# Scattering token rows to expert slots in the dense stage, and turning rows by DMA instead of TensorE, in a two-layer recurrent block

## The chip, the cores and the metric

The kernel runs on one NeuronCore of a Trainium2 chip. The metric is the device time of one execution in microseconds; the kernel before was timed three times, and one more execution was profiled. TensorE is written PE (its weight loads PEld), VectorE DVE, ScalarE ACT, GpSimd POOL, and SyncE, which issues most of the DMAs, SP.

## The reference

Layer 0 takes 8192 token rows of 256 numbers, normalises them, and runs linear attention (keys and values are summed into one small matrix per batch of 2048 tokens) beside a mixture of 16 experts: each token goes to its two best experts and also through one shared expert. Layer 1 is a retention attention and a feed-forward layer with FP4 quantised weights and activations. The change touches only layer 0:

```python
scores = softmax(xt @ gate_w.T); top_w, top_i = top_k(scores, 2)
# step over the 16 experts, for the tokens that chose this one:
a = silu(x @ W1.T + b1) * (x @ W3.T + b3)        # 127 numbers
h = concat([sqrt(sum(a*a) + 1), a])               # 128 numbers
s = h @ W2.T + b2                                 # 255 numbers
out = concat([sqrt(sum(s*s) + 1), s])             # one row of 256 per token and expert
```

The shared expert is the same computation with an inner width of 256. The attention that reads the key-value sums follows these stages, and a later stage combines for each token its two expert rows (found through `pos_lo` and `pos_hi`, the slots of the token).

## The kernel before

The core works through phases; each ends by clearing its semaphores and a barrier of all engines (`Phase.clear`). Within a phase every engine has a stream of its own, made by `pipeline`: at step s an engine runs, in the listed order, `stage(s - skew)` for each pair (skew, stage). An engine executes its list strictly in order, and stages of different engines meet through semaphores: `done(t)` waits until stage t of the other engine has finished, `free(t)` until the buffer that tile t - 2 used is free (two buffers, `LAG` = 2). Floats are kept as two float16 halves (hi and lo), and a product is three matmuls (`split3`).

Phases around the change, in their order:

- `weights0` loads and splits weights, and POOL fills constants; SP's later copies wait for all fills.
- `phase_norm` normalises the tokens, writes them as float16 halves to `x16_dram` (1 KB for each token) and holds them turned (features on partitions) in `xT_all`.
- `phase_route` chooses the experts and gives each (token, expert) pair a slot. Slots are sorted by expert, and each expert's slots are padded to a multiple of 128: 144 tiles of 128 slots. DVE does all of it in some 50 steps, each waiting for the one before; PE counts once in between.
- `phase_dense`, 64 tiles of 128 tokens: keys, values and key-value sums, and the shared expert (project, square and square root, `turn` on PE, copy `hidden_T` on DVE, `down`, then `z_out` on ACT and a store to `z_dram`). Beside it POOL runs `times` (a clamp at L1202 and a power at L1205, for the inner row of one tile and the outer row of an earlier one) and `scatter`: two indirect DMAs (L1212) that write token numbers, 4 bytes each, to `perm_dram` at the tokens' slots. SP loads a 381.5 KB expert weight pack every four tiles (`expert_load`).
- `phase_perm` reads that list back, PE turns it, and DVE converts it to indices in `perm_T`; DVE also makes the masked key-value matrices for the attention.
- `phase_experts`, 72 pairs of slot tiles: POOL gathers 2 x 128 rows of `x16_dram` by `perm_T` (two indirect DMAs, L1316), PE turns them with 8 transposes, DVE copies them out of PSUM (`rows_T`, L1457), PE projects with the expert's weights (a register holds which expert, `value_load`), ACT and DVE make the inner row, POOL the power (L1331), ACT and DVE split it, PE turns it with 4 transposes, DVE copies (`hidden_T`), PE projects down, ACT copies out, and SP stores 256 KB to `rows_dram`.
- `phase_attention`, `phase_combine`, and layer 1. Layer 1's `phase_norm_fp4` and `phase_ffn` already turn rows by DMA (`dma_start_transpose`, L451, L455, L772), from SBUF to SBUF.

Of the kernel before, what the change touches and what calls it, by code (L numbers as in the profile page):

```python
# [54 lines left out]
EXPERT_TILES = 2  # L55
EXPERT_LAG = 6
# [804 lines left out]
def phase_route(nc, ps, scores, consts, w_lo, w_hi, pos_lo, pos_hi, tile_expert):  # L861

    tri, ones, rev, tile_start = consts
    with Phase(nc, "route") as ph:
# [10 lines left out]
        s_step, s_hit, s_cnt = ph.sems("step hit cnt")  # L877
# [4 lines left out]
        over_n = lambda v: v.unsqueeze(1).to_broadcast([P, TILES, E])  # L882

# [11 lines left out]
        def _(dve):  # L895
# [23 lines left out]
            step(dve.tensor_tensor(a[:], c1[:], c2[:], ALU.is_gt))  # L919
            step(dve.tensor_scalar(b[:], a[:], -1.0, 1.0, ALU.mult, ALU.add))  # L920
            step(dve.tensor_tensor(w_lo[:], a[:], m1[:], ALU.mult))
            step(dve.tensor_tensor(w_hi[:], b[:], m1[:], ALU.mult))
            step(dve.tensor_tensor(c1[:], b[:], m2[:], ALU.mult))
            step(dve.tensor_tensor(c2[:], a[:], m2[:], ALU.mult))
            step(dve.tensor_tensor(w_lo[:], w_lo[:], c1[:], ALU.add))
            step(dve.tensor_tensor(w_hi[:], w_hi[:], c2[:], ALU.add))
# [10 lines left out]
            step(dve.tensor_tensor_scan(pinc[:], ones_f[:, 0:E], pad[:], 0.0, ALU.mult, ALU.add))  # L937
            step(dve.tensor_tensor(shift[:], pinc[:], pad[:], ALU.subtract))
# [24 lines left out]
def phase_dense(nc, ps, xT_all, w0, bias, ones2, khalf, kv_sum, pos_lo, pos_hi, tok_id, perm_dram, z_dram, e_dram, E16, late):  # L963

# [3 lines left out]
    ZLAG = 5  # L968
    with Phase(nc, "dense") as ph:
# [8 lines left out]
        hs16 = ph.sb("hs16", [P, LAG, 2, D], F16)  # L978
        hT = ph.sb("hT", [P, LAG, 2 * C, P], F16)
# [4 lines left out]
        zero_rows = ph.sb("zero_rows", [P, SLOT_TILES])  # L984
        (s_kv, s_sh, s_ke, s_kr, s_vhi, s_th, s_vlo, s_kp, s_u, s_s, s_khi, s_sq, s_klo, s_time, s_hhi, s_hlo,
         s_kvs, s_kvadd, s_turn, s_hT, s_z, s_zc, s_zsq, s_fill, s_pass, s_te, s_zfill, s_clear, s_kmax) = ph.sems(
            "kv sh ke kr vhi th vlo kp u s khi sq klo time hhi hlo kvs kvadd turn hT z zc zsq fill pass te zfill clear kmax")
# [3 lines left out]
        s_scat = ph.slot_sems("scat")  # L991
# [3 lines left out]
        turned = ps[:, 5, 0:D].bitcast(F16).rearrange("p (c m) -> p c m", m=P)  # L995
# [4 lines left out]
        def _(sp):  # L1000
            sp.wait_ge(s_zfill, 2)
            sp.dma_start(perm_dram.rearrange("(p t) o -> p (t o)", p=P), zero_rows[:]).then_inc(s_clear, 16)

            def store(t):
                sp.wait_ge(s_zc, done(t))
                through(sp, s_pass)
                sp.wait_ge(s_time, t.n + ZLAG + LAG + 1)
                sp.dma_start(token_tiles(z_dram)[t.n], zs[t.slot]).then_inc(s_store[t.slot], 16)

            def expert_load(t):  # L1010
                if t.slot4 == 0:
                    if not isinstance(t.n, int) or t.n > 0:
# [7 lines left out]
        def _(pe):  # L1020
            prime(pe, s_kv, s_sh, s_kvs, s_turn, s_z)
# [30 lines left out]
            def turn(t):  # L1052
                pe.wait_ge(s_hlo, done(t))
                pe.wait_ge(s_hhi, done(t))
                pe.wait_ge(s_hT, prev(t))
                for part in range(2):
                    for c in range(C):
                        ins = pe.transpose(turned[:, part * C + c], hs16[:, t.slot, part, c * P:(c + 1) * P],
                                           khalf[0][:])
                ins.then_inc(s_turn, 1)  # L1060

            def down(t):
                pe.wait_ge(s_hT, done(t))
                pe.wait_ge(s_zc, free(t))
                pe.wait_ge(s_zsq, free(t))
                for c in range(C):
                    split3(pe, zp[t.slot], (hT[:, t.slot, c], hT[:, t.slot, C + c]),
# [3 lines left out]
            pipeline(pe, TILES, [(6, down), (3, kv_product), (0, project), (4, turn)], 4)  # L1071

        @block.scalar
        def _(act):
            prime(act, s_vhi, s_ke, s_kr, s_th, s_khi, s_sq, s_hhi, s_zc, s_zsq)
            act.wait_ge(s_zfill, 2)
# [25 lines left out]
            def hidden_hi(t):  # L1102
                act.wait_ge(s_time, done(t))
                act.wait_ge(s_turn, free(t))
                act.activation(hs16[:, t.slot, 0], hs[t.slot], ACT.Copy).then_inc(s_hhi, 1)
# [15 lines left out]
            pipeline(act, TILES, [(7, z_out), (10, expert_hi), (3, hidden_hi), (2, key_hi), (1, nonlinear)], 4)  # L1121

        @block.vector
        def _(dve):
            prime(dve, s_vlo, s_kmax, s_kp, s_u, s_s, s_klo, s_hlo, s_hT)
# [4 lines left out]
            dve.memset(zero_rows[:], 0.0).then_inc(s_zfill, 1)  # L1130
# [25 lines left out]
            def hidden_lo(t):  # L1156
                dve.wait_ge(s_hhi, done(t))
                dve.tensor_tensor(hs16[:, t.slot, 1], hs[t.slot], hs16[:, t.slot, 0], ALU.subtract).then_inc(s_hlo, 1)
# [9 lines left out]
            def hidden_T(t):  # L1168
                dve.wait_ge(s_turn, done(t))
                dve.wait_ge(s_z, free(t))  # L1170
                dve.tensor_copy(hT[:, t.slot], turned).then_inc(s_hT, 1)

            def expert_lo(t):
                if t.slot4 == 0:
# [4 lines left out]
                                  (5, hidden_T),  # L1179
# [6 lines left out]
        def _(pool):  # L1186
            prime(pool, s_te, s_time)
            pool.memset(sums2[:], 0.0).then_inc(s_zfill, 1)
            pool.wait_ge(s_clear, 16)
# [1299 lines left out]
```

## Time and profile before

| what | us |
|---|---|
| three timed runs | 2192.92, 2199.99, 2200.06 (median 2199.99) |
| the profiled execution: its time, its span | 2197.53, 2195.8 |
| PE, DVE, ACT, POOL busy over the span | 1440.7 (66%), 1627.3 (74%), 1172.8 (53%), 1193.1 (54%) |
| `phase_route`, first to last DVE instruction | 129.0 to 171.2 |
| `phase_dense`, up to the barrier | 173 to 454.8 |
| `phase_perm` | 454.8 to 462.4 |
| `phase_experts` | 462.4 to 790 |

The trace can be asked for the busy time of each engine in a stretch (windows), for the instructions in order of time (timeline), for groups of instructions by line with what ended the idle time ahead of them (groups), for one source line, for the waits, and for the DMA queues of a stretch. "Issue" as a releaser means that the engine waited for nothing that the profile shows. Queue q1 carries SP's DMAs, q0 the indirect ones of POOL. DMA shares are of the core's 16 DMA engines.

### The profile page before, as it was taken

The numbers are of one execution on the slowest core, as the hardware profiler recorded it, in microseconds if no ns is written. First come the engines' busy times: TensorE is split into PE (matmuls) and PEld (weight loads), VectorE is DVE, ScalarE is ACT, GpSimd is POOL, SyncE is SP. The second block draws the span as 40 slices with busy tenths as digits, with TensorE's granted clock in tenths as the row PEclk, the third lists the DMA queues.
The fourth block names the chain that finished last, engine by engine and source line by source line (L and its number), as shares of the span: only waits on it lengthen the run. The fifth ranks groups of instructions, "written<-read, shape, count | busy, mean of one in ns | idle before, by whom it ended". The sixth has DMA issues, their size and how long they took to land. (4 is left out here: it accounts for less than half of the span.)

```text
span 2195.8 us, 69028 instructions
## 1 busy us (share of the span) xinstructions
PE 1440.7 (66%) x23272; PEld 1048.3 (48%) x23273; DVE 1627.3 (74%) x3726; ACT 1172.8 (53%) x3124; POOL 1193.1 (54%) x1188
## 2 busy tenths in 40 slices
PE   1628999947777879800000003999999679999846
PEld 1514666536666659700000001766666446666634
DVE  5887778735555557567666996999999558888778
ACT  3515777726666669724433553444444357777611
POOL 3206777757777645588871552222222257777745
PEclk9999999979999989955555556999999899999878
DMA  4501222223344410045664774333333312222236
GB/s 151 170 29 23 59 53 54 61 67 123 124 124 124 113 40 0 31 148 182 190 182 143 159 155 83 65 61 66 62 63 66 75 38 53 53 53 53 49 103 204
DMA packets 299437, 200.33 MB, mean 91 GB/s; under 512 B 177788, under 2 KB 287310, under 8 KB 299342
## 3 DMA queue, kind: packets, MB, share of 16 engines
q1 hardware_dynamic: 282192, 163.45, 29.1%
q0 software_dynamic: 17152, 35.74, 5.9%
q8 instruction: 46, 0.75, 0.2%
q14 instruction: 47, 0.39, 0.1%
HBM read 89.89 MB, written 52.60 MB: 65 GB/s over the span
## 5 line engine op out<-in xcount | busy, mean ns | idle before, releaser
L192 PE MATMUL ps<-all_late,l_xq_T 128*128 128x352 f16 x1536 | 244.4, 317 | 294.8 <-DVEq L180 285.4
L192 PEld LDWEIGHTS ps<-all_late,l_xq_T 128*128 (+1 forms) x1536 | 148.2, 99 | 385.4 <-DVEq L180 285.6
L642 POOL TENSOR_TENSOR ffn_h<-ffn_fq_val,ffn_h 128x704 f16<-128x704 f32 x64 | 97.4, 1521 | 285.0 <-ACT ffn_h L637 285.0
L192 PE MATMUL ps<-l_W,all_xT_all 128*128 128x16 f16 (+2 forms) x1152 | 205.2, 315 | 66.7 <-ACT all_xT_all L375 40.3
L1316 POOL DMA_INDIRECT experts_g<-x_dram,l_perm_T x144 | 142.0, 986 | 76.0 <-issue 57.7
L192 PEld LDWEIGHTS ps<-l_W,all_xT_all 128*128 (+1 forms) x1152 | 95.6, 101 | 152.2 <-issue 28.4
L810 ACT ACTIVATE ffn_th<-ps 128x352 f32<-128x352 f32 x128 | 59.3, 463 | 194.5 <-PE ps L192 194.5
L2174 POOL TENSOR_TENSOR all_late<-ret_pm,all_late 128x512 f16<-128x512 f32 x128 | 145.4, 1157 | 19.3 <-ACT all_late L2080 19.3
L796 PE MATMUL ps<-all_late,ffn_hT 128*128 128x256 f16 x1088 | 130.9, 275 | 7.2 <-ACT l_xq_T L820 4.4
L796 PEld LDWEIGHTS ps<-all_late,ffn_hT 128*128 128x128 f16 x1088 | 106.9, 99 | 26.2 <-issue 4.9
L192 PE MATMUL ps<-moe_E,experts_gT 128*128 x864 | 114.9, 273 | 0.0
L192 PE MATMUL ps<-moe_E,experts_hT 128*128 x432 | 70.9, 279 | 59.8 <-issue 54.8
L2102 DVE TENSOR_TENSOR ret_pm<-ps,tables_causal 128x1024 f32<-128x1024 f32 x64 | 78.4, 1225 | 42.2 <-PE ps L1947 29.7
L192 PE MATMUL ps<-l1b_W,all_xT_all 128*128 128x512 f16 x384 | 97.8, 394 | 10.4 <-DVEq L1870 10.4
L1331 POOL TENSOR_TENSOR experts_rows<-experts_se,all_mhalf 128x4 f32<-128x4 f32 (+1 forms) x77 | 78.4, 1018 | 38.5 <-DVE experts_se L1446 23.3
L2062 ACT ACTIVATE all_late<-ps,tables_parity 128x512 f16<-128x512 f16 x128 | 81.3, 694 | 10.8 <-PE ps L1962 10.7
L1701 POOL DMA_INDIRECT combine_ob<-rows_dram,moe_pos_hi x64 | 75.5, 1180 | 19.5 <-issue 19.5
L192 PEld LDWEIGHTS ps<-moe_E,experts_gT 128*128 128x128 f16 x864 | 81.6, 98 | 9.4 <-issue 0.4
L1701 POOL DMA_INDIRECT combine_oa<-rows_dram,moe_pos_lo x64 | 70.4, 1100 | 18.2 <-issue 17.5
L1451 DVE TENSOR_SCALAR experts_se<-experts_so 128x2 f32<-128x2 f32 x72 | 13.7, 190 | 89.2 <-ACT all_late L1431 85.7
L1212 POOL DMA_INDIRECT perm_dram<-moe_tok_id,moe_pos_lo x64 | 69.7, 1089 | 17.1 <-issue 12.6
L2043 ACT ACTIVATE all_xT_all<-ps 128x256 f32 (+1 forms) x64 | 24.5, 383 | 100.0 <-PE ps L2007 100.0
(302 smaller groups left out, 4839.3 us busy)
## 6 DMA issues: line engine op xcount, KB each, us to landing
rows_dram<-experts_rows SPq DMA_DIRECT2D x72, 256.0 KB
ret_v<-ret_vpad SPq DMA_DIRECT2D x256, 64.0 KB
normA_xin<-x SPq DMA_DIRECT2D x16, 512.0 KB
x_dram<-normA_x SPq DMA_DIRECT2D x16, 512.0 KB
z_dram<-dense_rows SPq DMA_DIRECT2D x64, 128.0 KB
combine_xin<-x SPq DMA_DIRECT2D x16, 512.0 KB
combine_zin<-z_dram SPq DMA_DIRECT2D x16, 512.0 KB
x_dram<-combine_sig SPq DMA_DIRECT2D x16, 512.0 KB
```

The lines of the kernel that those rows point to most:

```text
L192: mm = pe.matmul(out, lhs[a], rhs[b], start=first and n == 0, stop=last and n == 2, skip_group_check=True)
L642: eng.tensor_tensor(lo, self.shaped(t, hi), hi, ALU.subtract).then_inc(self.lo, 1)
L796: ins = pe.matmul(down_ps[t.slot], hT[:, t.slot4, c % both], DN[:, c], start=c == 0, stop=c == both + FFC - 1, skip_group_check=True)
L810: act.activation(th[:, t.slot, k], gate[k], ACT.Silu, scale=1 / WS).then_inc(s_th[k], 1)
L1212: pool.indirect_dma_start(perm_dram, bass.IndirectOffsetOnAxis(ap=pos[:, t.n:t.n + 1], axis=0), tok_id[:, t.n:t.n + 1], None).then_inc(s_s ...
L1316: pool.indirect_dma_start(g16[:, t.slot, k], None, x16_dram, bass.IndirectOffsetOnAxis(ap=perm_T[:, t.n * U + k:t.n * U + k + 1], axis=0)) ...
L1331: pool.tensor_tensor(rows[:, u, which, :, 0], se[:, u, which], power[:, which], ALU.pow).then_inc(s_time, 1)
L1701: pool.indirect_dma_start(dst[:, t.slot4, k], None, rows_dram, at).then_inc(arrived[t.slot], 16)
L2043: act.activation(yT_all[:, bass.ds(t.n, 1)].rearrange("p o c m -> p (o c) m"), yps, ACT.Copy, scale=1 / Y_SCALE).then_inc(s_yev, 1)
L2062: ins = act.activation(kx16[:, t.slot4].rearrange("p a c s e j -> p (a c s) e j")[:, :, e], src, ACT.Copy, scale=parity[:, e:e + 1])
L2102: dve.tensor_tensor(pm[:, t.slot4], sps, causal[:].unsqueeze(1).to_broadcast([P, 4, RC]), ALU.mult).then_inc(s_p, 1)
L2174: ins = pool.tensor_tensor(p16[:, u, 1, r], pm[:, u, r], p16[:, u, 0, r], ALU.subtract)
```

## The change

- The dense stage no longer scatters token numbers. SP loads the token's 128 x 1 KB rows again from `x16_dram` (`rows_in`, four buffers), and POOL scatters these rows, twice, straight to `slots_dram` (1 KB for each slot). `phase_perm`, `perm_T` and the gathers are gone.
- Padding slots get zeros: 2 MB beyond the last possible token slot by two plain DMAs at the start of `phase_route`, and for each expert its last 128 slots by two indirect DMAs of 128 rows of 8 KB, as soon as DVE has the padded counts. Eight small DVE operations on the weights `w_lo` and `w_hi` move behind that point, and four operations are new. POOL fills the 4096 zero columns in `weights0`.
- The expert stage reads its rows turned, straight from `slots_dram`, by one DMA transpose for each pair of tiles (256 rows of 512 halves) issued by SP. The inner rows of both stages are also turned by a DMA transpose (128 x 512, SBUF to SBUF). All buffers that these fill are fourfold. PE's transposes and DVE's copies out of PSUM are gone.
- The squares of the inner row move from ACT to DVE in the expert stage, and the masked key-value matrices are made by DVE at the start of the expert stage.
- SP's list is fixed and in order: dense `turn`, `rows_in`, `expert_load`, `store`; experts `turn_hidden`, `turn_rows`, `store`.

```diff
@@ phase_route
+        @block.sync
+        def _(sp):
+            beyond = slots_dram[TOK * TOPK:SLOT_TILES * P].rearrange("(p k) d -> p (k d)", p=P)
+            width = zeros.shape[1]
+            for k in range(beyond.shape[1] // width):
+                sp.dma_start(beyond[:, k * width:(k + 1) * width], zeros).then_inc(s_beyond, 16)
+            sp.wait_ge(s_beyond, 16 * (beyond.shape[1] // width))
+        @block.gpsimd
+        def _(pool):
...
+            pool.wait_ge(s_last, 1)
+            for k in range(2):
+                pool.indirect_dma_start(slots_dram.rearrange("(r k) d -> r (k d)", k=PAD_ROWS),
+                                        bass.IndirectOffsetOnAxis(ap=last_at[:, k:k + 1], axis=0), zeros,
+                                        None).then_inc(s_zeroed, 16)
+            pool.wait_ge(s_zeroed, 32)
@@ phase_dense
-    ZLAG = 5
+    ZLAG = 6
-            pipeline(sp, TILES, [(0, expert_load), (0, store)], 4)
+            def rows_in(t):
+                if t.n >= 4:
+                    sp.wait_ge(s_scat[t.n % 4], 32 * (t.n // 4))
+                sp.dma_start(x16[:, t.n % 4], token_tiles(x16_dram)[t.n]).then_inc(s_x16[t.n % 4], 16)
+            def turn(t):
+                sp.wait_ge(s_hlo, done(t))
+                if t.n >= 4:
+                    sp.wait_ge(s_z, t.n - 4 + LAG + 1)
+                sp.dma_start_transpose(hT[:, t.n % 4], hs16[:, t.n % 4].rearrange("p k d -> p (k d)")
+                                       ).then_inc(s_hT[t.n % 4], 16)
+            unrolled(TILES, [(7, turn), (0, rows_in), (11, expert_load), (12, store)])
-            pipeline(pe, TILES, [(6, down), (3, kv_product), (0, project), (4, turn)], 4)
+            pipeline(pe, TILES, [(7, down), (3, kv_product), (0, project)], 4)
-            pipeline(act, TILES, [(7, z_out), (10, expert_hi), (3, hidden_hi), (2, key_hi), (1, nonlinear)], 4)
+            pipeline(act, TILES, [(8, z_out), (10, expert_hi), (3, hidden_hi), (2, key_hi), (1, nonlinear)], 4)
             def scatter(t):
-                if t.n >= LAG:
-                    pool.wait_ge(s_scat[t.slot], 2 * slot_free(t))
-                    through(pool, s_pass)
+                pool.wait_ge(s_x16[t.n % 4], 16 * (t.n // 4) + 16)
+                through(pool, s_pass)
                 for pos in (pos_lo, pos_hi):
-                    pool.indirect_dma_start(perm_dram, bass.IndirectOffsetOnAxis(ap=pos[:, t.n:t.n + 1], axis=0),
-                                            tok_id[:, t.n:t.n + 1], None).then_inc(s_scat[t.slot], 16)
+                    pool.indirect_dma_start(slots_dram, bass.IndirectOffsetOnAxis(ap=pos[:, t.n:t.n + 1], axis=0),
+                                            x16[:, t.n % 4], None).then_inc(s_scat[t.n % 4], 16)
@@ phase_experts
+            def turn_rows(t):
+                if t.n >= 4:
+                    sp.wait_ge(s_up, t.n - 4 + LAG + 1)
+                sp.dma_start_transpose(gT[:, t.n % 4].rearrange("p c k m -> p c (k m)"), slots[t.n]
+                                       ).then_inc(s_gT[t.n % 4], 16)
+            def turn_hidden(t):
+                sp.wait_ge(s_hlo, done(t))
+                if t.n >= 4:
+                    sp.wait_ge(s_down, t.n - 4 + LAG + 1)
+                sp.dma_start_transpose(hT[:, t.n % 4].rearrange("p a k m -> p (a k) m"),
+                                       hs16[:, t.n % 4].rearrange("p a k m -> p (a k m)")).then_inc(s_hT[t.n % 4], 16)
-            pipeline(sp, count, [(0, store)])
+            unrolled(count, [(7, turn_hidden), (0, turn_rows), (11, store)])
-            pipeline(pe, count, [(10, experts_both), (4, experts_first), (10, down), (2, turn), (4, project), (8, turn2)])
+            pipeline(pe, count, [(EXPERT_LAG, experts_both), (0, experts_first), (EXPERT_LAG, down), (0, project)], 4)
-            pipeline(act, count, [(11, output), (7, hidden_hi), (6, square), (5, gate)])
+            pipeline(act, count, [(7, output), (3, hidden_hi), (1, gate)], 4)
-            pipeline(dve, count, [(11, out_clamp), (3, rows_T), (9, hidden_T), (6, hidden_clamp), (7, hidden_lo), (5, hidden)])
+            pipeline(dve, count, [(7, out_clamp), (2, square), (2, hidden_clamp), (3, hidden_lo), (1, hidden)], 4)
@@ weights0
+                                     (late[:, 0:PAD_ROWS * 2 * D], 0.0)],
```

## Rows read from the trace of the kernel before

**Rows 1.** Windows over the two stages: PE, PEld, DVE, ACT, POOL busy, PE clock, DMA share
```profile
172.00:447.00 275.00, 269.32 (x1920) 161.69 (x1920) 207.66 (x547) 202.91 (x713) 198.29 (x263) 0.99 0.23 52
...
473.00:768.00 295.00, 232.21 (x2364) 187.25 (x2365) 169.95 (x483) 175.34 (x749) 208.15 (x207) 0.99 0.40 119
```
**Rows 2.** Timeline of the dense stage, one tile: start, us, engine, line
```profile
321.99 0.39 PE L1058 MATMUL ps<-all_ident,dense_hs 128*128 128x128 f16 x4
...
322.21 0.82 PE L192 MATMUL ps<-l_W,dense_hT 128*128 128x255 f16 x6
...
323.79 0.22 POOL L1202 TENSOR_SCALAR dense_se<-dense_sums 128x2 f32<-128x2 f32 x1 [0.64 <-ACT all_late L1099]
...
326.39 0.95 POOL L1212 DMA_INDIRECT perm_dram<-moe_tok_id,moe_pos_hi  x1 [0.30 <-issue]
```
**Rows 3.** Timeline and SP waits at the end of the dense stage
```profile
444.57 0.36 SPq L1014 DMA_DIRECT2D dense_e_stage<-e_pack  x1
...
445.34 0.33 SPq L1008 DMA_DIRECT2D z_dram<-dense_rows  x1
...
448.28 0.38 ACT L1110 ACTIVATE dense_rows<-ps 128x255 f32<-128x255 f32 x1 [3.16 <-DMA z_dram<-dense_rows]
...
SPq L1017 <- DMA z_dram<-dense_rows: 1.2, 1, 1.2
```
**Rows 4.** Timeline from the barrier after the dense stage to the first expert projection
```profile
454.77 0.34 SPq L1237 DMA_DIRECT2D perm_pr<-perm_dram  x1
...
464.77 0.96 POOL L1316 DMA_INDIRECT experts_g<-x_dram,l_perm_T  x1 [0.31 <-issue]
...
467.53 1.03 PE L1363 MATMUL ps<-all_ident,experts_g 128*128 128x128 f16 x8 [8.89 <-DMA experts_g<-x_dram,l_perm_T]
...
474.25 1.48 PE L192 MATMUL ps<-moe_E,experts_gT 128*128 x6
```
**Rows 5.** Groups of the expert stage, 500 to 750 us: busy, mean ns, idle before
```profile
L1316 POOL DMA_INDIRECT experts_g<-x_dram,l_perm_T x120 | 118.6, 988 | 54.7 <-issue 49.2 <-DVE experts_se L1451 2.4 <-DVE experts_hs L1470 2.2
L1331 POOL TENSOR_TENSOR experts_rows<-experts_se,all_mhalf 128x4 f32<-128x4 f32 x60 | 62.6, 1043 | 15.6 <-DVE experts_se L1446 12.7 <-issue 1.5 <-DVE experts_hs L1470 1.2
...
L192 PE MATMUL ps<-moe_E,experts_hT 128*128 x355 | 56.8, 274 | 54.8 <-issue 50.9 <-DVE experts_hT L1475 3.0 <-ACT all_late L1431 0.8
```
**Rows 6.** DMA queues: feed-forward 1500 to 1700, experts 480 to 760, dense 190 to 430
```profile
q1 hardware_dynamic: 50878, 12.74, 34.1%
...
q0 software_dynamic: 6432, 17.57, 24.1%
q1 hardware_dynamic: 16864, 16.26, 17.1%
...
q1 hardware_dynamic: 9827, 12.33, 21.6%
```
**Rows 7.** The DMA transposes of layer 1, by line: SP's issue time, us to landing
```profile
L772 SPq DMA_TRANSPOSE ffn_hT<-ffn_h x64: 1367/1386/2525, 1367.4 to 1725.6; - x64
...
L451 SPq DMA_TRANSPOSE all_xT_all<-normB_x x16: 1778/1917/2147, 1195.6 to 1332.8; - x16
...
DMA to landing us min/median/max: 4.3/4.4/5.4
```
**Rows 8.** Timeline of weights0, the fill by POOL and the last split by DVE
```profile
0.84 7.74 POOL L227 MEMSET l_B<- 128x9165 f16 x1
...
11.53 0.29 DVE L239 SCALAR_TENSOR_TENSOR l_b<-weights_stage,l_b 65x141 f16<-65x141 f32 x1
```
**Rows 9.** Timeline of phase_route
```profile
145.67 1.06 PE L891 MATMUL ps<-route_hit,moe_ones 128*128 128x512 f16 x2
...
145.89 0.22 DVE L919 TENSOR_TENSOR route_a<-route_c 128x64 f32<-128x64 f32 x1
...
147.93 1.87 DVE L928 COPY route_total<-ps 128x1024 f32<-128x1024 f32 x1
...
170.96 0.19 DVE L960 CAST moe_tile_expert<-route_both 1x78 int32<-1x78 f32 x1
```

More of the change, by code:

```diff
@@ L960, in _, with phase_dense @@
             step(dve.tensor_copy(tile_expert[:], both[:]))
-def phase_dense(nc, ps, xT_all, w0, bias, ones2, khalf, kv_sum, pos_lo, pos_hi, tok_id, perm_dram, z_dram, e_dram, E16, late):
+def phase_dense(nc, ps, xT_all, w0, bias, ones2, half, kv_sum, pos_lo, pos_hi, x16_dram, slots_dram, z_dram, e_dram, E16, late):
     s13, s2 = 2 * SINTER, OUTW
-    ZLAG = 5
+    ZLAG = 6
     with Phase(nc, "dense") as ph:
@@ L1050, in kv_product @@
                 ins.then_inc(s_kvs, 1)
[L1052 to L1060, printed above, removed]
             def down(t):
-                pe.wait_ge(s_hT, done(t))
+                pe.wait_ge(s_hT[t.slot4], 16 * (t.n // 4) + 16)
                 pe.wait_ge(s_zc, free(t))
@@ L1282, in phase_experts @@
         se = ph.sb("se", [P, LAG, 2, U])
-        (s_pass, s_turn, s_gT, s_up, s_th, s_u, s_s, s_sq, s_te, s_time, s_hhi, s_hlo, s_turn2, s_hT, s_down,
-         s_oc, s_osq, s_teo, s_one, s_spass) = ph.sems(
-            "pass turn gT up th u s sq te time hhi hlo turn2 hT down oc osq teo one spass")
-        s_gather, s_store = ph.slot_sems("gather"), ph.slot_sems("store")
-        turned = [ps[:, u, :].bitcast(F16).rearrange("p (k c m) -> p k c m", k=U, m=P) for u in range(LAG)]
+        masked = late[:, LAG * 2 * U * D * 2:LAG * 2 * U * D * 2 + BATCH * C * KVW * 2].bitcast(F32).rearrange(
+            "p (b c k) -> p b c k", b=BATCH, c=C)
+        (s_up, s_th, s_u, s_s, s_sq, s_te, s_time, s_hhi, s_hlo, s_down, s_oc, s_osq, s_teo, s_one, s_pass,
+         s_step) = ph.sems("up th u s sq te time hhi hlo down oc osq teo one pass step")
+        s_store = ph.slot_sems("store")
+        s_gT, s_hT = ([ph.sem(f"{n}{u}") for u in range(4)] for n in ("gT", "hT"))
         hp = [ps[:, 2 + u, 0:U * up].rearrange("p (k n) -> p k n", k=U) for u in range(LAG)]
-        turned2 = ps[:, 4, 0:U * P].bitcast(F16).rearrange("p (c k m) -> p c k m", k=U, m=P)
         op = [ps[:, 5 + u, 0:U * OUTW].rearrange("p (k n) -> p k n", k=U) for u in range(LAG)]
@@ L1331, in times @@
                 pool.tensor_tensor(rows[:, u, which, :, 0], se[:, u, which], power[:, which], ALU.pow).then_inc(s_time, 1)
-            for n in range(count + 6 + OLAG):
-                if n >= 6:
-                    times(n - 6)
-                if n < count:
-                    gather(Tile(n, n % LAG, n // LAG))
+            for n in range(count + OLAG):
+                times(n)
         @block.tensor
         def _(pe):
-            prime(pe, s_turn, s_up, s_turn2, s_down)
+            prime(pe, s_up, s_down)
             held = {}
```

237 lines of the change are left out of this document (88 added, 149 removed).

## The prediction

> **What bounds the kernel now.** I read the busy shares first: no engine carries the whole span, so the stages the change touches have to be priced one by one. The windows [rows 1] show the dense stage bound by PE: 269.3 of 275 us busy for 64 tiles, 4.2 us a tile. The expert stage isn't: PE 232 of 295 us. Its groups [rows 5] show POOL: two gathers of 0.99, a power of 1.04, and per pair (54.7 + 15.6) / 60 = 1.17 us of idle, nearly all "issue", together 4.2 us a pair; over the stage 295 / 72 = 4.1. The timeline between the stages [rows 4] shows a third piece: 474.25 - 454.77 = 19.5 us from the barrier to the first expert projection, for building the index list, its barrier, the first gathers, and turning. PE runs at its full clock (0.99) in both stages.
>
> **Route and weights.** POOL's new fill of 4096 columns costs 7.74 x 4096 / 9165 = 3.5 us [rows 8], so POOL finishes at 12.0; SP waits anyway for DVE's last split, which ends at 11.8: +0.3. In the route, PE's counts are ready at 145.67 + 1.06 = 146.7. Today eight small DVE operations fill 145.9 to 147.9, 2.04 us [rows 9]. After, DVE idles until 146.8 (1.1 earlier than the copy starts today), does four new operations of 0.2, then the eight: -1.1 + 0.8 + 2.0 = +1.7 us. The padding counts are ready near 155, and DVE's last operation is at 171, now 173. The zero scatters (two descriptor generations of 1 us, 2 MB) must fit into 17 us: SP's stores of the expert stage move 16.26 MB in 17.1% of 280 us [rows 6], 340 GB/s, so 2 MB take 6 us and a landing of 2. Hidden; without that cover, up to 10 us.
>
> **Dense stage, gains.** PE loses four transposes, 322.21 - 321.99 = 0.22 us a tile [rows 2], giving 3.98. DVE and ACT are at 75% of the window and lose work or keep it. POOL issues as many indirect DMAs; descriptor generation of 128 rows costs it 0.99 for 1 KB rows [rows 5] and 0.95 for 4-byte ones [rows 2], so nothing is added: from the clamp to the end of the second scatter 326.39 + 0.95 - 323.79 = 3.55 us, plus the 0.30 that stands between two of its instructions, 3.85. It is just below PE.
>
> **Dense stage, a new loop.** SP's list is in order, and `rows_in(s)` waits for the scatters of tile s - 4 to land; `store(s - 12)` is queued behind it. POOL's `times` at its step p needs the store of tile p - 10 landed (two z buffers). That store is in SP's step p + 2, behind the wait for the scatter of POOL's step p - 2. So two POOL steps hold this ring: POOL 3.55; scatter landing 1.8 (a gather pair: 464.77 + 0.96 to 467.53 [rows 4]); SP's load issue 0.35; store from issue to landing 0.33 + 1.2 [rows 3]; three semaphore hops of 0.1, my estimate, below the 0.30 of idle between two scatters [rows 2]; and the load's data ahead of the store. A 1 KB row costs 24.1% x 280 x 16 / (134 gathers x 128) = 63 ns of one DMA engine [rows 6], so 128 rows take 0.5 us on 16. Sum 8.0, or 4.0 a tile. Once in four tiles the 381.5 KB weight load goes ahead of the store: then store to landing is 448.28 - 445.34 = 2.94 instead of 1.5 [rows 3], plus 0.36 of issue: (16.1 + 1.8) / 4 = 4.46 a tile. DMA work per tile becomes 21.6% x 4.2 = 0.9 today [rows 6], + 0.5 load, + 1.0 scatters, + 0.7 transpose (below) = 3.1 us of 4.2, so landings lengthen somewhat. Bounds: 3.98 (PE alone, -14 us) to 5.0 (each landing 0.5 later, +51 us). I take 4.4: 64 x 0.2 = +13 us. The drain gains a step and DMA round trips of two or three us: +3.
>
> **Between the stages.** The index phase goes. After the barrier SP issues one transpose of 1024 packets. The like of it [rows 7]: 2048 packets of 256 bytes take 1.9 us of issue and land 4.4 us after; the feed-forward stage pays 34.1% x 200 x 16 / 50878 = 21.4 ns a packet [rows 6], so 2048 are 2.7 us of data and the rest, 1.7, is fixed. For 1024: 1.4 + 1.7 = 3.1, and with barrier and hops 4.1 us to the first projection: -15.4. The masked key-value matrices, which today fit inside the index phase (7.6 us in the table), now occupy DVE at the start of the stage; its first needed work comes only when the first projection has ended, at about 5.5 us, so nothing is charged; without that cover they would cost what they take, under 7.6 us.
>
> **Expert stage.** POOL keeps one power a pair, 1.04 + waits, and is out. PE: 232.2 / 72 = 3.23 busy less twelve transposes at 0.22 / 4, 0.66, plus 50.9 / 60 = 0.85 of "issue" ahead of the down projection (the register work on the expert numbers, which stays): 3.42. DVE (2.4 a pair) loses two copies and gains two squares; ACT (2.4) loses two squares; both stay below PE. SP issues per pair a transpose of 512 columns, one of 1024 and a store: issue is 1.37 for 1408 columns and 1.92 for 2048 [rows 7], so about 0.6 + 1.05 + 0.38 = 2.0. DMA: transposes 1536 x 21.4 / 16 = 2.05, the store 17.1% x 280 / 62 = 0.77: 2.8 of 3.4 us. The unknown is the 1024-packet transpose that reads HBM: no row shows one. From below the SBUF price, 21.4 ns; from above the 63 ns of a gathered HBM row, which gives (1024 x 63 + 512 x 21.4) / 16 + 0.77 = 5.5 us a pair. The nearest row is the transpose, in packet size and in its turning; I take about 25 ns, DMA 3.05, and a pair of 3.5 us with PE and DMA both near full: 72 x (3.5 - 4.1) = -43 us. The feedback is slack: SP's `turn_hidden(s - 6)` follows `project(s - 4)`, `turn_rows` and a store, about 5.5 us, and PE needs it after three periods, 10 us. Tail +1.
>
> Of packets of 256 bytes, the trace has only the SBUF price, 187 GB/s: 12.74 MB in 34.1% of 200 us [rows 6]. The Trainium skill (DMA: Bandwidth & Descriptors, Why small descriptors are slow (HBM only)) puts the overhead of a 256-byte HBM packet at 27%, which speaks against the change: by it the packet is 27 ns, and DMA needs 3.2 us a pair, against which PE would still bound. The Trainium skill (Advanced Engine Details and Errata, X-Bar Transpose (TRN2)) gives transposes 350 to 400 GB/s; the trace shows about half of that, and by the page DMA would need only 1.9 us.
>
> **Sum.** 0.3 + 1.7 + 13 + 3 - 15.4 - 43 + 1 = -39.4. The profiled execution took 2197.5, 2.5 below the median of the runs, which is within their spread: 2197.5 - 39.4 = **2158 us**. I take 0.5%, 11 us, as the least that a measurement of this kernel tells from no change.
>
> **Rivals.**
> - *A. HBM transposes are dear.* If a packet from HBM costs 40 ns or more, DMA holds the pair: (1024 x 43 + 512 x 21.4) / 16 + 0.77 = 4.2 us at twice the SBUF price. The expert stage then gains nothing (+7 instead of -43), and the total is 2208; at 63 ns, 5.5 a pair, +101 us and 2302. It turns slower from about 40 ns, a pair of 4.05 us. For it: gathers of HBM rows take 63 ns apiece. Against: those rows are four times as long, 63 / 4 = 16 ns per 256 bytes. Chance 0.24.
> - *B. The dense loop costs all of its upper bound.* At 5.0 us a tile the dense stage loses 51 instead of 13, and the total is 2196. For it: SP's list puts the store behind the scatter's landing, and DMA rises from 22% to 75%. Against: the ring without the weight load is no longer than PE's own 4.0. Chance 0.14.
> - *C. Both stages at PE's pace.* Dense at 3.98 (-14) and experts at 3.3 (-58): 2116. For it: fourfold buffers. Against: the weight load in SP's list. Chance 0.10.
> - *D. No expert gain because PE's register work grows* to fill its idle time, since it was read as 0.85 while PE was never pressed: at 4.0 a pair, 2194. Chance 0.04.
>
> The forecast itself gets 0.48, and its own range is 2125 to 2188. The range of 8 in 10 holds it, C, B, D, and A up to 52 ns: **2112 to 2250**. Faster by over 0.5%: the forecast, C, a third of B and D: 0.64. Within: parts of A, B and D, 0.13. Slower: most of A and a little of B, 0.23.
>
> **What the profile after would show.** Dense: PE busy below 95% of the stage, tiles 4.3 to 4.5 us apart, the gap longest once in four tiles, POOL's clamp waiting for the DMA of `z_dram`. If tiles are 4.0 apart the loop never bound; if POOL waits for `x16` instead, the load is what is late. First expert projection 4 us after its phase begins. Experts: pairs 3.4 to 3.6 us apart, PE busy over 70%, DMA share 0.8 to 0.95, and q1 holding about 1000 more small packets a pair; PE waiting for `gT` with DMA near 1.0 means rival A. What would make me wrong most: the price of the HBM transpose, then the issue time of a transpose on SP, which if it is 1.5 us instead of 1.05 makes SP's list 2.5 us, still covered.

## The result, and the profile of the changed kernel

The changed kernel takes 2232.29 us (median of four runs, 2226.86 to 2233.8), the kernel before 2198.4 on the same chip (median of four): a ratio of 1.0154, with a 95% interval from 1.0128 to 1.018. It is slower by 1.5%, where the prediction had it faster at 2158. The time lies inside the predicted range, where only rival A would have put it (2208 to 2302). That is luck: rival A's reason is not what the runs show.

The gain and the loss lie in two neighbouring stages, so the windows come first. Columns as in [rows 1]; the stretches are the dense stage and the expert stage after.

```profile
175.00:505.00 330.00, 271.44 (x1630) 145.27 (x1628) 183.66 (x477) 191.37 (x699) 200.47 (x254) 0.96 0.51 142
...
526.00:804.00 278.00, 195.86 (x1535) 125.29 (x1534) 133.30 (x628) 127.57 (x466) 70.84 (x70) 0.99 0.71 159
```

Against [rows 1], PE fell from 98% busy (269.32 of 275) to 82% of a dense stage that is now longer, and no other engine took its place: DVE, ACT and POOL are at 56, 58 and 61%, DMA at half. Where nothing is full, something waits in a circle. The expert stage is shorter, and nothing is full there either (PE 70%, DMA 0.71).

Where the time went, from the first and last ACT exponential of the dense stage, the first DMA transpose of slots, the first and last projection of the expert stage and the first ACT instruction of the attention, in both traces:

| piece | before | after | difference | predicted |
|---|---|---|---|---|
| start of the dense stage | 178.7 | 180.6 | +1.9 | +2.0 |
| dense, 63 tile periods | 178.7 to 437.3 | 180.6 to 502.1 | +62.9 | +13 |
| drain, up to the barrier | 17.5 | 19.8 | +2.3 | +3 |
| barrier to the first expert projection | 19.5 | 3.8 | -15.7 | -15.4 |
| expert stage, first to last projection | 293.7 | 278.4 | -15.3 | -43 |
| tail, up to the attention | 25.7 | 26.2 | +0.5 | +1 |

That is +36.6 in sum. The span goes from 2195.8 to 2231.2, +35.4, so the stages behind hold their lengths to about a microsecond. Four of the six terms came out within a microsecond; two missed, one by 50 us and one by 28.

**The dense stage.** The waits, first those of the engines and then SP's own (engine, line, what it waited for; microseconds in all, times, longest), from 190 to 490 us:

```profile
ACT dense_rows L1131 <- DMA z_dram<-dense_rows: 106.0, 44, 5.3
DVE dense_hs L1178 <- ACT dense_hs L1126: 95.0, 44, 5.8
POOL dense_se L1216 <- ACT all_late L1120: 78.5, 43, 5.3
...
SPq L1027 <- DMA slots_dram<-all_late,moe_pos_hi: 158.0, 51, 5.1
```

SP waits 158 us for scatters to land before it loads the next token rows, ACT waits for a store that stands behind that load in SP's list, and POOL, which issues the scatters, waits for ACT. That is a ring. The timeline of one turn of it, with POOL, SP and ACT put together (start, duration, engine, line; idle before, and what ended it):

```profile
340.42 0.23 POOL L1216 TENSOR_SCALAR dense_se<-dense_sums 128x2 f32<-128x2 f32 x1 [3.26 <-ACT all_late L1120]
...
343.03 0.96 POOL L1225 DMA_INDIRECT slots_dram<-all_late,moe_pos_hi  x1 [0.30 <-issue]
...
345.45 0.33 SPq L1027 DMA_DIRECT2D all_late<-x_dram  x1
345.87 0.38 SPq L1039 DMA_DIRECT2D z_dram<-dense_rows  x1
346.35 1.20 SPq L1033 DMA_TRANSPOSE dense_hT<-dense_hs  x1
...
347.94 0.38 ACT L1131 ACTIVATE dense_rows<-ps 128x255 f32<-128x255 f32 x1 [2.36 <-DMA z_dram<-dense_rows]
348.22 0.38 ACT L1134 ACTIVATE all_late<-ps 128x255 f32<-128x255 f32 x1
...
348.58 0.42 ACT L1126 ACTIVATE dense_hs<-dense_rows 128x256 f16<-128x256 f32 x1
348.88 0.42 ACT L1116 ACTIVATE dense_k<-dense_kp 128x256 f16<-128x256 f32 x1
349.19 0.41 ACT L1120 ACTIVATE all_late<-dense_rows 128x255 f32<-128x255 f32 x1
349.49 0.20 ACT L1120 ACTIVATION_READ_ACCUMULATOR all_late<-dense_rows 128x1 f32 x1
...
349.88 0.22 POOL L1216 TENSOR_SCALAR dense_se<-dense_sums 128x2 f32<-128x2 f32 x1 [0.94 <-ACT all_late L1120]
```

Read it as a sum. POOL's clamp to the end of its second scatter is 343.99 - 340.42 = 3.57. The scatter lands and SP issues the load at 345.45: 1.46. SP issues the store 0.42 later. The store lands and ACT writes `z_out` at 347.94: 2.07. ACT then goes through its list, outer square, `hidden_hi`, `key_hi`, inner square, up to 349.69: 1.75. POOL's clamp follows 0.19 later. The whole is 9.46 us, and POOL has done two tiles in it.

Every other turn holds the weight load. Its SP and ACT rows, one turn earlier:

```profile
333.76 0.34 SPq L1027 DMA_DIRECT2D all_late<-x_dram  x1
334.15 0.42 SPq L1045 DMA_DIRECT2D dense_e_stage<-e_pack  x1
334.68 0.37 SPq L1039 DMA_DIRECT2D z_dram<-dense_rows  x1
...
338.49 0.38 ACT L1131 ACTIVATE dense_rows<-ps 128x255 f32<-128x255 f32 x1 [3.95 <-DMA z_dram<-dense_rows]
```

Here the store takes 338.49 - 334.68 = 3.81 instead of 2.07, and the two clamps around this turn stand at 328.44 and 340.42, 11.98 apart. Four tiles cost 9.46 + 11.98 = 21.4, or 5.36 each. POOL's clamps from 200 to 500 us are 5.31 apart on average; over all 63 periods a tile takes 5.10, because the first seven clamps, before there is a store to wait for, follow each other 3.7 apart.

**Between the stages.** After the barrier:

```profile
521.89 5.28 SPq L1271 DMA_TRANSPOSE experts_gT<-slots_dram  x4
...
525.67 1.45 PE L193 MATMUL ps<-moe_E,experts_gT 128*128 x6 [9.54 <-DMA experts_gT<-slots_dram]
```

3.8 us where [rows 4] had 19.5.

**The expert stage.** DMA queue, and its landings, from 550 to 780 us, with the waits of the same stretch:

```profile
q1 hardware_dynamic: 106196, 37.24, 70.1%
...
experts_gT<-slots_dram SPq DMA_TRANSPOSE x57, 3.3
experts_hT<-experts_hs SPq DMA_TRANSPOSE x57, 2.4
...
ACT experts_rows L1373 <- DMA rows_dram<-experts_rows: 125.1, 57, 5.2
```

A packet costs 0.701 x 230 x 16 / 106196 = 24.3 ns on average. A pair has 106196 / (230 / 3.869) = 1786 of them. Taking out 256 of the store at 45 ns (17.1% x 280 x 16 / 16864 of [rows 6]) and 512 from SBUF at 21.4 leaves about 20 ns for a packet that the transpose reads from HBM. This is an estimate: it supposes that the prices of the other two hold here. By it the transpose from HBM was not dear; what ACT waits for, in nearly every pair, is the store of the pair before last, 125 us in 230: that transfer is queued in SP's list behind both transposes.

### The profile page after: what moved, and what is told of

The parts are those of the page before. It is cut to its first block and busy times, and to the rows that moved or that the text cites. A ratio compares the mean times of both kernels' runs of the same rounds, so it can differ in the third digit from the quotient of the medians.

```text
span 2231.2 us, 65393 instructions
## 1 busy us (share of the span) xinstructions
PE 1412.1 (63%) x22150; PEld 971.2 (44%) x22151; DVE 1565.1 (70%) x3808; ACT 1117.6 (50%) x2836; POOL 1060.0 (48%) x1049
## 5 line engine op out<-in xcount | busy, mean ns | idle before, releaser
L193 PE MATMUL ps<-l_W,all_xT_all 128*128 128x16 f16 (+2 forms) x1152 | 216.1, 327 | 82.7 <-ACT all_xT_all L376 40.3
L1373 ACT ACTIVATE experts_rows<-ps 128x510 f32<-128x510 f32 x72 | 42.8, 595 | 147.9 <-DMA rows_dram<-experts_rows 145.2
L1178 DVE TENSOR_TENSOR dense_hs<-dense_rows,dense_hs 128x256 f16<-128x256 f32 x64 | 27.2, 424 | 108.6 <-ACT dense_hs L1126 97.9
L193 PEld LDWEIGHTS ps<-moe_E,experts_gT 128*128 128x128 f16 x864 | 71.3, 98 | 67.3 <-issue 48.7
L1131 ACT ACTIVATE dense_rows<-ps 128x255 f32<-128x255 f32 x64 | 24.6, 385 | 129.3 <-DMA z_dram<-dense_rows 111.3
L1652 POOL DMA_INDIRECT combine_ob<-rows_dram,moe_pos_hi x64 | 75.5, 1179 | 19.5 <-issue 19.5
L1225 POOL DMA_INDIRECT slots_dram<-all_late,moe_pos_hi x64 | 71.5, 1118 | 21.0 <-issue 19.5
```

What stands on the lines that cost most here:

```text
L193: mm = pe.matmul(out, lhs[a], rhs[b], start=first and n == 0, stop=last and n == 2, skip_group_check=True)
L1178: dve.tensor_tensor(hs16[:, t.slot4, 1], hs[t.slot], hs16[:, t.slot4, 0], ALU.subtract).then_inc(s_hlo, 1)
L1225: pool.indirect_dma_start(slots_dram, bass.IndirectOffsetOnAxis(ap=pos[:, t.n:t.n + 1], axis=0), x16[:, t.n % 4], None).then_inc(s_scat[t. ...
L1373: act.activation(os[t.slot][:, :, 1:D], op[t.slot], ACT.Copy, scale=1 / WS).then_inc(s_oc, 1)
L1652: pool.indirect_dma_start(dst[:, t.slot4, k], None, rows_dram, at).then_inc(arrived[t.slot], 16)
```

## The experiments

Ratios are to the kernel before on the same chip, with 95% intervals. Its median was 2205.32 beside the first four kernels here, 2195.32 beside the next four and 2200.68 beside the last four, so kernels of different groups are compared by their ratios. "Tile" is the mean of the 63 periods of the dense stage. "Pair" is the time from the start of the first projection of the expert stage to the end of the last, divided by its 72 pairs.

| run | what | us | ratio | tile | pair |
|---|---|---|---|---|---|
| before | | | 1 | 4.105 | 4.085 |
| after | | 2232.29 | 1.0154 [1.0128, 1.018] | 5.103 | 3.869 |
| e1_store_first | dense: store ahead of the load | 2187.72 | 0.9932 [0.9908, 0.9955] | 4.384 | 3.854 |
| e2_eight_buffers | dense: eight row buffers | 2163.37 | 0.982 [0.9793, 0.9848] | 4.06 | 3.841 |
| e3_experts_store_first | experts: store first | 2221.76 | 1.0085 [1.0061, 1.0109] | 5.129 | 3.757 |
| e4_both_store_first | e1 and e3 | 2180.02 | 0.9892 [0.9868, 0.9916] | 4.411 | 3.769 |
| e5_eight_and_store | e2 and e3 | 2146.8 | 0.9774 [0.9755, 0.9793] | 3.889 | 3.752 |
| e6_fixed_experts | e5, experts not chosen | 2107.17 | 0.9599 [0.9583, 0.9615] | 3.873 | 3.202 |
| e7_dense_pe_turn | e5, dense turn on PE | 2162.41 | 0.9854 [0.9837, 0.987] | 4.07 | 3.755 |
| e8_act_order | after, ACT's list reordered | 2218.25 | 1.0105 [1.0088, 1.0122] | 4.873 | 3.833 |
| e9_changed_again | after | 2232.94 | 1.0145 [1.0127, 1.0164] | 5.097 | 3.855 |
| e10_pe_turn_ring | after, dense turn on PE | 2234.02 | 1.015 [1.0133, 1.0167] | 5.146 | 3.858 |
| e11_store_later | after, dense store a step later | 2491.5 | 1.1325 [1.1297, 1.1353] | 9.168 | 3.839 |
| e12_both_again | e5 | 2147.79 | 0.9766 [0.9749, 0.9782] | 3.91 | 3.766 |

The theory for the dense stage is the ring. Its rivals are that the added DMA work makes every landing long (contention), that SP's issue time for the transposes is what holds it, and that POOL's scatters of rows are dearer than those of numbers.

### The ring cut at either of two places

e1 issues the store ahead of the load, so that it no longer stands behind the scatter's landing:

```diff
-            unrolled(TILES, [(7, turn), (0, rows_in), (11, expert_load), (12, store)])
+            unrolled(TILES, [(7, turn), (11, expert_load), (12, store), (0, rows_in)])
```

> One edit to the changed kernel: in the dense stage's SP list the z store stands ahead of rows_in, so it no longer waits for a scatter to land. Ring theory: the changed kernel's two-tile ring is 9.46 us (POOL clamp to end of second scatter 3.57, scatter landing 1.46, load issue 0.42, store landing 2.07, ACT's order z_out, splits and inner square 1.75, hop 0.19); with the store ready at the end of the power it is about 5.5, and PE (3.98) or POOL (3.85) bound a tile. Dense projections go from 5.08 us a tile to 4.0 to 4.3, total 2232 to between 2162 and 2182, faster than the kernel before by 1 to 1.7%. Rival, DMA contention (dense DMA share rose from 0.23 to 0.52, each landing is longer whatever the order): the same bytes move, so 5 us a tile stays and the total is above 2215.

e2 leaves the order and makes the wait one for the scatter of eight tiles before (the same 8 for 4 stands in the buffer, the semaphores and POOL's waits, left out here):

```diff
-                if t.n >= 4:
-                    sp.wait_ge(s_scat[t.n % 4], 32 * (t.n // 4))
-                sp.dma_start(x16[:, t.n % 4], token_tiles(x16_dram)[t.n]).then_inc(s_x16[t.n % 4], 16)
+                if t.n >= 8:
+                    sp.wait_ge(s_scat[t.n % 8], 32 * (t.n // 8))
+                sp.dma_start(x16[:, t.n % 8], token_tiles(x16_dram)[t.n]).then_inc(s_x16[t.n % 8], 16)
```

> The other way to cut the same ring, leaving SP's order: eight x16 buffers instead of four, so rows_in(s) waits for the scatter of tile s - 8, long landed, and the store behind it isn't held. Ring theory: as in the run with the store first, 4.0 to 4.3 us a tile in the dense stage, total 2162 to 2185, SP's wait on slots_dram (158 us in 300) near zero. Contention rival: total above 2215.

e2 came out as expected: 4.06 us a tile, and the total is 1.8% under the kernel before. All transposes, scatters and stores are still there, so neither their issue time on SP nor POOL's work nor the amount of DMA work costs the 63 us. In its windows, from 190 to 430 us, and its waits, PE is busy 96% and DMA is busier than in the changed kernel (0.63 against 0.51):

```profile
190.00:430.00 240.00, 230.74 (x1512) 131.73 (x1510) 166.26 (x438) 181.85 (x651) 181.18 (x237) 1.00 0.63 180
...
ACT dense_rows L1131 <- DMA z_dram<-dense_rows: 17.4, 13, 2.4
```

SP no longer waits for `slots_dram` there at all. e1 gained as well (4.384 a tile), but less than I expected (4.0 to 4.3, and at most 2182 us in all where it took 2187.72); SP's wait for the scatters is still there, and it now stands ahead of the next `turn` and the next store:

```profile
SPq L1027 <- DMA slots_dram<-all_late,moe_pos_hi: 45.0, 20, 4.7
```

Here the reordered list moved the wait, and the deeper buffers took it away.

### The ring lengthened, and its inside changed

e11 changes one number: the store of the dense stage goes one step later in SP's list. By the ring, the store that POOL's step p needs is then behind the scatter of step p - 1 instead of p - 2, and the same 9.46 us hold for one tile.

```diff
-            unrolled(TILES, [(7, turn), (0, rows_in), (11, expert_load), (12, store)])
+            unrolled(TILES, [(7, turn), (0, rows_in), (11, expert_load), (13, store)])
```

> The changed kernel with the dense store one SP step later (skew 13 for 12), nothing else. Ring theory: the store of tile p - 10 is now in SP's step p + 3, behind the scatter of POOL's step p - 1, so the same chain of 9.5 us holds one tile instead of two: the dense stage goes to 9 to 9.6 us a tile, the total to about 2232 + 64 x 4.2 = 2500 (2470 to 2530). Contention rival: the same work and bytes, one tile of lag more: within 15 us of the changed kernel.

The tile took 9.168 us and the kernel 2491.5. The mean holds the quick start and end of the stage: between 200 and 750 us the tiles are 10.03 apart. The ring gives that too, once the weight load is counted, which was left out of the expectation: three turns of 9.46 and one of 11.98 make 10.1 a tile. Nothing was added to any engine or queue; DMA share falls to 0.28 while PE is busy 60%:

```profile
190.00:430.00 240.00, 143.46 (x688) 69.44 (x686) 76.31 (x199) 77.69 (x283) 84.78 (x107) 0.79 0.28 81
```

e10 keeps the ring whole and gives the dense inner rows back to PE and DVE, which takes the 512-column transposes off SP and off the DMA engines (PE's turn and DVE's copy themselves are left out here):

```diff
-            unrolled(TILES, [(7, turn), (0, rows_in), (11, expert_load), (12, store)])
+            unrolled(TILES, [(0, rows_in), (11, expert_load), (12, store)])
...
-            pipeline(pe, TILES, [(7, down), (3, kv_product), (0, project)], 4)
+            pipeline(pe, TILES, [(7, down), (3, kv_product), (0, project), (4, turn)], 4)
```

> The changed kernel with the dense stage's inner rows turned by PE and DVE again, the four buffers and SP's order of rows_in, load and store as in the change: the ring is whole, but the DMA transposes beside it are gone (DMA share of the dense stage from 0.52 to about 0.35). Ring theory: the ring holds no transpose, so tiles stay 4.9 to 5.1 us apart and the total within 15 us of the changed kernel. Contention rival: the landings shorten with the traffic, the tile falls to 4.6 or below, 30 us or more faster.

Its windows beside the changed kernel's, both from 190 to 430 us (the changed kernel's in the second fence):

```profile
190.00:430.00 240.00, 204.99 (x1364) 116.73 (x1363) 145.91 (x386) 136.01 (x503) 137.17 (x183) 0.95 0.37 116
```

```profile
190.00:430.00 240.00, 198.28 (x1192) 106.30 (x1191) 131.75 (x343) 138.83 (x509) 145.10 (x186) 0.95 0.51 142
```

DMA share fell from 0.51 to 0.37, SP issues a third less, and the tile stayed where it was (5.146 against 5.097). Contention and SP's issue time are out as causes of the dense loss.

e8 tests the leg that I had left out, ACT's. It puts the inner square's stages ahead of `z_out`, so that POOL's clamp no longer waits for the inner square behind it:

```diff
-            pipeline(act, TILES, [(8, z_out), (10, expert_hi), (3, hidden_hi), (2, key_hi), (1, nonlinear)], 4)
+            pipeline(act, TILES, [(3, hidden_hi), (2, key_hi), (8, z_out), (10, expert_hi), (1, nonlinear)], 4)
```

> The changed kernel with one edit in the dense stage: ACT splits and squares the inner rows before z_out instead of after it. In the ring as the profile shows it, 1.0 to 1.1 us of ACT work (hi of the hidden row, hi of the key, inner square) stands between the z store's landing and POOL's clamp; with it ahead of the wait the ring is 8.4 us instead of 9.46, and a tile 4.55 to 4.8 instead of 5.08: -18 to -32 us. If the ring doesn't pass through ACT's order (POOL waits for the store itself, as the prediction had it), nothing changes, within 5 us.

It gained 0.22 us a tile, 14 us in the stage by the profiled executions, and about 0.4% in all, where 18 to 32 us were expected. The waits from 190 to 430 us show why:

```profile
POOL dense_se L1216 <- ACT all_late L1134: 56.6, 32, 4.4
ACT dense_k L1116 <- DVE dense_kp L1170: 33.0, 45, 1.1
```

POOL's clamp takes two sums in one instruction, and the outer one (L1134) is still behind the store; and `key_hi`, moved forward, now comes before DVE has its input. Of the 1.75 us of ACT's leg, `z_out`'s copy and outer square are 0.74 (347.94 to 348.68) and can't be moved ahead of the store; the order of the list could give back the other 1.01 at most. That the ACT leg belongs to the ring is shown by the gain and by the new releaser. That it is worth all of its 1.75 us is read from the timeline; no run took it away whole.

### The expert stage

e3 does in the expert stage what e1 does in the dense one:

```diff
-            unrolled(count, [(7, turn_hidden), (0, turn_rows), (11, store)])
+            unrolled(count, [(11, store), (7, turn_hidden), (0, turn_rows)])
```

> Only the expert stage's SP list: the store of rows_dram ahead of the two transposes. Ring theory for this stage: ACT's output waits for the store of two pairs before (125 us in 230), which stands behind a wait on DVE's low half and behind 2.5 us of transpose issue. With the store first the pair goes from 3.87 us to PE's 3.4 to 3.5: -25 to -32 us, total 2200 to 2207. Rival, PE's register work or the DMA engines (share 0.70) hold the pair: less than 8 us, total above 2224.

ACT's wait for the store fell from 125.1 us to this:

```profile
ACT experts_rows L1373 <- DMA rows_dram<-experts_rows: 8.7, 6, 2.7
...
L193 PE MATMUL ps<-moe_E,experts_hT 128*128 x354 | 57.4, 274 | 62.1 <-issue 59.0 <-ACT all_late L1375 3.0
```

but the pair only went from 3.869 to 3.757, where 3.4 to 3.5 was expected. The group's second part says what is under it: 59.0 us of "issue" ahead of the down projection in 230 us, about 1.0 for each pair. PE is not kept by another engine there. What stands there in PE's list is register work, a load and a row of divisions that give the expert numbers for `project` and `down`; e6 tests below whether it is that.

e4 puts e1 and e3 together.

> Both stores first. Ring theory: the two gains add, -60 and -28: total about 2145 (2130 to 2160), 2 to 3% faster than the kernel before. If contention or PE hold either stage, it equals the better of the two single runs.

It is e1's tile (4.411) and e3's pair (3.769), and missed its expectation for the same two reasons.

e5 puts e2 and e3 together, and e12 runs it once more beside the changed kernel.

> Eight x16 buffers in the dense stage and the store first in the expert stage's SP list. Both gains are of different stages and should add: ratio 0.982 of the one and the 12 to 17 us of the other give about 0.975 of the kernel before, some 2150 us. If the expert stage's gain was an accident of where the dense stage ended, it stays at 0.982.

> The kernel with eight x16 buffers and the experts' store first once more, on the chip of the changed kernel's run: 0.977 of the kernel before, 3.7 to 4% faster than the changed kernel.

Both gave the same: 2146.8 and 2147.79, 2.3% under the kernel before, and e12 is 85 us, 3.8%, under the changed kernel (e9) of the same group. In e12's dense stage PE is busy 98% at full clock:

```profile
190.00:430.00 240.00, 235.69 (x1568) 136.68 (x1566) 174.68 (x456) 189.40 (x676) 190.65 (x244) 1.00 0.68 186
```

e6 takes e5 and leaves out the choice of the expert: PE uses the weights of experts 3 and 9 for every pair, so the register work is gone and the matmuls are the same in number and size.

```diff
-                v = pe.value_load(tile_expert[0:1, bass.ds(n, 1)], min_val=0, max_val=E ** (2 * U) - 1)
-                held["project"] = [v // E ** k % E for k in range(U)]
-                held["down"] = [v // E ** (U + k) % E for k in range(U)]
+                held["project"] = [3, 9]
+                held["down"] = [3, 9]
```

> The run with eight buffers and the store first, but PE takes experts 3 and 9 for every pair, so that it loads and divides no register (the choice of the expert is left out). With the store first, a pair of the expert stage takes 3.76 us: 2.67 of PE busy and about 1.0 of PE's own issue. Theory PE: register work is the bound, the pair falls to 2.8 to 3.1 us, 45 to 65 us less than the same kernel with the registers. Rival, DMA or SP: the DMA engines' share is 0.74 of the stage and SP issues three transfers in 3.1 us, so the pair stops at 3.5 or above and less than 20 us is gained.

The pair fell from 3.752 to 3.202, 40 us in 72 pairs; 2.8 to 3.1, 45 to 65 us, was expected. The windows from 530 to 680 us and the waits from 520 to 690:

```profile
530.00:680.00 150.00, 118.36 (x1008) 92.96 (x1006) 86.69 (x414) 86.60 (x320) 46.54 (x46) 1.00 0.83 197
...
ACT experts_rows L1372 <- DMA rows_dram<-experts_rows: 70.4, 52, 1.9
```

With the register work gone ACT waits for the store again and DMA is at 0.83 (0.72 in e12), so the next bound lies there and not in PE, which is busy 79%. No run separates the store's wait from the DMA engines' load.

e7 takes e5 and turns the dense inner rows on PE, as the kernel before does (the edit is that of e10). It asks what the DMA transposes of the dense stage bring once the ring is open.

> The run with eight buffers and the store first, with one part of the change undone: the dense stage's inner rows are turned by PE (four transposes) and copied by DVE again, and SP issues no dense transpose. If PE is what bounds the dense stage once the ring is cut, each tile costs 0.22 us more, 4.06 to 4.28, +14 us. If SP's list or DMA traffic holds it, the undone part costs nothing or gains: within 4 us or faster.

It is 15.6 us slower than e5, for 14 expected. PE is full, 4.07 us a tile:

```profile
190.00:430.00 240.00, 239.99 (x1739) 145.09 (x1738) 184.85 (x495) 182.52 (x647) 188.14 (x235) 1.00 0.44 146
```

e9 is the changed kernel once more.

> The changed kernel itself once more, beside the runs of this call, so that they are compared on one chip: 1.0154 of the kernel before within its interval.

It repeated the first result, 1.0145 and 1.0154.

## Why the prediction was wrong

**Route, weights, drain, the gap, tail: right.** The start moved by 1.9 us for 2.0 predicted. The zero scatters were hidden, as said: POOL issues the first at 156.25, and the last DVE operation of the route now starts at 172.73 (170.96 in [rows 9]), with POOL long done.

```profile
156.25 1.22 POOL L899 DMA_INDIRECT slots_dram<-all_late,route_last_at  x1 [42.52 <-DVE route_last_at L954]
...
172.73 0.19 DVE L985 CAST moe_tile_expert<-route_both 1x78 int32<-1x78 f32 x1
```

The gap went from 19.5 to 3.8 us. The masked matrices cost nothing visible.

**"A new loop": the mechanism right, its length wrong.** This is the step that failed and that turned the sign. The loop was found, with the waits it goes through, but its sum was 8.0 us for two tiles where the trace has 9.46, and 9.9 with the weight load where it has 11.98. Term by term: POOL 3.55 predicted, 3.57 measured. Scatter landing 1.8, measured 1.46. SP's load issue 0.35, measured 0.42. Store from issue to landing, with the load's data ahead of it, 1.53 + 0.5 = 2.03, measured 2.07. All of these were good. The three hops of 0.3 are not seen by themselves: all but the last, 0.19 from ACT to the clamp, lie inside the measured terms. The term that was not there is ACT, which the prediction put at nothing without a reason: I wrote that POOL needs the store landed and let POOL go on from there. But POOL's clamp needs two sums that ACT makes, and ACT's `z_out` waits for the same store. The outer sum comes with `z_out`, and the inner one is behind it in ACT's in-order list, with `hidden_hi` and the first half of `key_hi` between: 1.75 us in all. The sign was in the profile after: the prediction would have POOL's clamp wait for the DMA of `z_dram`, and it waits for ACT's inner square (78.5 us above). The weight load was undersized too: the store behind it took 3.81, where the prediction has 2.94 + 0.5 = 3.44. In place of (16.1 + 1.8) / 4 = 4.46 stands 21.4 / 4 = 5.36, above even the upper bound of 5.0, which had stretched landings and not looked for a further leg. 1.0 us more for each of 63 tiles is the 62.9 of the table. (The predicted +13 counted from 4.2 a tile, PE's share of a window; the periods of before are 4.105 apart, so 4.4 should have been +19. PE's floor was off in the same way: 4.105 less the turn's 0.22 is 3.89, not 3.98, and e5 has 3.889.)

Rival B, which priced the loop at 5.0, was near for the dense stage (51 lost predicted, 63 measured), but by luck: its price came from landings 0.5 longer each, and the scatter's and the store's landing were no longer than predicted (1.46 and 2.07). Its total, 2196, rested on the expert gain of 43.

**"I take 4.4" had no room.** It lies under the prediction's own sum of 4.46, although PE's margin over the loop (3.98 against 4.0) was nil by the prediction's own numbers, so that each microsecond missing from the loop would show at half its size in every tile.

**Expert stage: the disputed price right, the bound wrong.** The HBM transpose came to about 20 ns a packet, the estimate above, for 25 predicted, and DMA works 0.701 x 3.869 = 2.7 us a pair for 3.05. Rival A, at 40 and more, is refuted: by its price DMA alone would need 4.0 us a pair, and a pair took 3.87, in e6 3.20. The Trainium skill (DMA: Bandwidth & Descriptors, Why small descriptors are slow (HBM only)) gives 3 cycles of overhead in 11 for a 256-byte packet from HBM; on 21.4 ns that is 29, an estimate (the prediction multiplied by 1.27 and had 27), and the trace is below both. The Trainium skill (Advanced Engine Details and Errata, X-Bar Transpose (TRN2)) gives 350 to 400 GB/s; the trace of before shows about half, 187 GB/s. The pair is 3.869 and not 3.5 for two reasons. First, "the feedback is slack" looked at the transposes and not at the store: ACT's output waits for the store of two pairs before, and that store stands in SP's list behind a wait for DVE's low half and two transposes, whose issue is longer than I had, 1.21 for 512 columns (1.20 in the dense stage) where 0.6 was estimated and 1.29 for 1024 packets where 1.05 was:

```profile
L1033 SPq DMA_TRANSPOSE dense_hT<-dense_hs x64: 1194/1196/2118, 188.4 to 507.6; - x64
...
L1271 SPq DMA_TRANSPOSE experts_gT<-slots_dram x72: 1227/1290/1318, 521.9 to 790.4; - x72
...
L1278 SPq DMA_TRANSPOSE experts_hT<-experts_hs x72: 1192/1206/1852, 534.5 to 812.2; - x72
```

e3 gives this back: 0.11 us a pair. Second, PE's own pace, 3.42 in the prediction, is 3.76 (e3, e5, e12). The windows of e12 from 550 to 700 us, and of the same stretch the group that the idle time stands ahead of:

```profile
550.00:700.00 150.00, 105.45 (x835) 66.79 (x833) 71.62 (x342) 75.18 (x266) 38.45 (x38) 1.00 0.72 165
...
L193 PE MATMUL ps<-moe_E,experts_hT 128*128 x228 | 36.9, 274 | 41.3 <-issue 41.3
```

The busy part was nearly right, 3.23 - 0.66 = 2.57 predicted and 105.45 / 150 x 3.77 = 2.65 here. It is the idle time that was read as 0.85 and is (150 - 105.45) / 150 x 3.77 = 1.12, of which 41.3 / 38 = 1.09 is "issue" ahead of the down projection. That it was partly hidden before is argued, not shown. That is rival D, given 0.04: smaller than its 4.0, but there. e6 shows that it is this register work, by taking it away.

**What in the profile could have told.** The store's other user is in [rows 3]: ACT's `z_out` shows 3.16 us of idle ended by the DMA of `z_dram`. I used that row for the landing time and didn't ask what stands behind `z_out` in ACT's list.

**Still open.** Why e2's tile is 4.06 and that of e5 and e12 3.89 and 3.91, with the same dense code: the first ran on another chip than the others, and nothing in the runs tells whether that or something else is behind it. How much of the change's total comes from each part is measured only for the dense turn (e7); the scattering of rows and the turning from `slots_dram` were not tried apart.

## What to carry to other kernels

A buffer that one engine fills and another frees through an in-order list ties that list's other entries to it: when a wait is put ahead of a store, follow the store to every engine that waits for it, and then down each of their lists to what is queued behind that wait, until the circle closes; only then add it up and divide by the tiles in flight. If the loop is as long as the bound to within a few per cent, try deeper buffers first: here they took the whole loss away, and reordering the list only part of it. And an engine's "issue" time read while it had slack can be too low: 0.85 a pair before, 1.0 to 1.1 once PE was pressed.

## What the runs showed of the hardware

- The issue of a DMA transpose holds SP for 1.20 us at 128 x 512 halves from SBUF, 1.29 at 256 x 512 from HBM, and 1.39 and 1.92 in [rows 7]. In packets of 256 bytes that is 512, 1024, 1408 and 2048: from 512 to 1408 the issue grows by 0.2 us only.
- Turning rows out of HBM was no dearer per packet than out of SBUF, about 20 ns (the estimate above) against 21.4, and landed 3.3 us after its issue began (from SBUF, for half the packets, 2.4).
- The second scatter of a tile, 128 rows, took POOL 0.96 us of descriptor generation whether a row has 4 bytes ([rows 2], 0.95) or 1 KB, with occasional ones of 1.69. SP, which waits for its landing, went on 1.46 us after it (1.75 in the turn with the weight load).
- The granted clock of PE fell where the ring starved it: 0.99 before in the dense stage ([rows 1]), 0.95 in the changed kernel with PE 83% busy, 0.79 in e11 with 60%, and 1.00 again in e12 with 98%.
